# GpSimd's order between two blocks of a transformer layer, and scores for maxima one PSUM bank at a time

## The reference

```python
xn = _layernorm(x)
# attention over windows of 64 rows, 16 heads of 16 values, each window sees 3
scores = where(mask, einsum('bnqhd,bnkhd->bhnqk', q, kc) * scale, -1e9)
out = einsum('bhnqk,bnkhd->bnqhd', softmax(scores), vc) @ Wo + bo
h = layer_norm(out + xn, g1, b1)
f = gelu(h @ W1 + c1) @ W2 + c2
attn = layer_norm(f + h, g2, b2)
# routing: each row goes through the one expert with the largest score
chosen = argmax(xn @ gate_w.T)
moe = xn + xn @ expert_w[chosen].T
return x + attn + moe
```

## Time and profile before

| what | before |
|---|---|
| median of 3 runs (lowest to highest) | 1473.32 us (1461.51 to 1473.76) |
| the profiled execution | 1471.13 us, span 1469.3 us |
| PE busy | 1200.0 us, 82% |
| VectorE busy | 924.3 us, 63% |
| ScalarE busy | 726.5 us, 49% |
| GpSimd busy | 825.5 us, 56% |
| chain that ended last | PE 42%, GpSimd 26%, issue 12%, VectorE 7% |
| granted TensorE clock, mean | 0.928 |

### The profile page before, as it was taken

The page is one execution under the profiler, slowest core; times in us unless marked ns, Lnnn a source line. Parts: engine busy times, 40 slices in busy tenths (PEclk is TensorE's granted clock), DMA queues, the critical chain, the costliest instruction groups (busy, mean ns, idle before and its releaser), DMA issues.

```text
span 1469.3 us, 32444 instructions
## 1 busy us (share of the span) xinstructions
PE 1200.0 (82%) x11720; PEld 726.1 (49%) x11720; DVE 924.3 (63%) x2207; ACT 726.5 (49%) x1355; POOL 825.5 (56%) x1088
## 2 busy tenths in 40 slices
PE   0717898799879898898987898798986989878877
PEld 0414454554637445464545546374454645365445
DVE  8554657476656746776575766577474765656455
ACT  1304657146562574436572575526763365725661
POOL 6551568435781567625674457815676266834664
PEclk9958999899989899999998999898998999999989
DMA  8443081231723254230812327231532408122010
GB/s 250 120 130 116 31 199 50 80 127 44 163 76 104 73 132 99 72 125 31 199 51 80 126 59 156 69 109 67 147 85 72 124 32 202 54 85 87 3 29 29
DMA packets 93977, 142.89 MB, mean 97 GB/s; under 512 B 10592, under 2 KB 62688, under 8 KB 91744
## 3 DMA queue, kind: packets, MB, share of 16 engines
q1 hardware_dynamic: 87680, 124.04, 30.6%
q0 software_dynamic: 6144, 16.79, 3.6%
HBM read 74.47 MB, written 68.29 MB: 97 GB/s over the span
## 4 chain that ended last, share of the span: by engine, by line
PE 42%; POOL 26%; issue 12%; DVE 7%; ACT 3%; DMA 3%; another core or an unknown queue 0%; DVEq 0%; POOLq 0%; SPq 0%; ACTq 0%
PE bank L1180 6%; PE bank L1268 5%; PE bank L1078 5%; PE bank L1081 5%; PE bank L1079 5%; PE bank L1173 4%; POOL x_sb L521 4%; DVE m_sb L745 4%; POOL xs_dram L507 4%; POOL res_r L527 3%; POOL pool L496 3%; POOL pool L499 3%; POOL x_sb L483 3%; POOL x_sb L480 3%; PE bank L1148 2%
## 5 line engine op out<-in xcount | busy, mean ns | idle before, releaser
L981 ACT ACTIVATE pool<-bank 128x512 f32<-128x512 f32 x512 | 285.5, 596 | 150.9 <-PE bank L1180 147.5
L745 DVE TENSOR_REDUCE m_sb<-bank 128x2 f32<-128x384 f32 x512 | 261.5, 552 | 130.3 <-PE bank L1188 128.7
L468 POOL TENSOR_SCALAR_AFFINE_SELECT pool<-pool 128x512 f32<-128x512 f32 x256 | 183.6, 717 | 244.1 <-ACT pool L981 205.5
L1180 PE MATMUL bank<-q_s,k_s 128*128 128x256 f16 x1024 | 185.1, 289 | 15.7 <-ACT pool L981 8.8
L412 POOL TENSOR_TENSOR rs<-ve,neghalf 128x1 f32<-128x1 f32 x64 | 36.9, 577 | 251.7 <-DVE ve L806 251.7
L1268 PE MATMUL bank<-pool,v_a 128*32 128x256 f32 (+2 forms) x2560 | 166.7, 352 | 8.4 <-POOL pool L473 8.3
L970 ACT ACTIVATE xn<-bank 128x256 f32<-128x256 f32 x120 | 46.0, 384 | 224.4 <-PE bank L1081 218.6
L1173 PE MATMUL bank<-k_s,q_s 48*64 48x192 f16 x2048 | 99.1, 270 | 58.9 <-DVE m_sb L745 40.5
L1180 PEld LDWEIGHTS bank<-q_s,k_s 128*128 128x128 f16 x1024 | 82.5, 101 | 126.3 <-issue 97.4
L820 DVE TENSOR_TENSOR pool<-pool 128x512 f16<-128x512 f32 x128 | 105.5, 827 | 62.1 <-ACT pool L995 52.7
L473 POOL TENSOR_SCALAR_AFFINE_SELECT pool<-pool 128x512 f32<-128x512 f32 x208 | 133.4, 641 | 0.0
(11 more groups left out here) (154 smaller groups left out, 2644.6 us busy)
## 6 DMA issues: line engine op xcount, KB each, us to landing
pair_dram<-pool SPq DMA_DIRECT2D x96, 256.0 KB, 4.2
xn<-xs_dram SPq DMA_DIRECT2D x40, 384.0 KB, 3.6
ys_dram<-xn SPq DMA_DIRECT2D x120, 128.0 KB, 1.8
q_s<-pair_dram SPq DMA_DIRECT2D x32, 384.0 KB, 6.7
k_s<-pair_dram SPq DMA_DIRECT2D x32, 384.0 KB, 8.3
x_sb<-in_L_attn_x SPq DMA_DIRECT2D x8, 1024.0 KB, 5.8
res_dram<-x_sb SPq DMA_DIRECT2D x8, 1024.0 KB, 5.2
res_r<-res_dram SPq DMA_DIRECT2D x8, 1024.0 KB, 5.0
```

The source lines that it names most:

```text
L468: nc.gpsimd.affine_select(out=p, in_=p, compare_op=ALU.is_ge, fill=0.0, base=0, pattern=[[0, 4], [1, 2 * W]], channel_multiplier=-1).then_ ...
L745: nc.vector.tensor_reduce(m_sb[:, 4 * g + par:4 * g + 4:2, t], SB[par][:, 0:2 * WIN].rearrange("p (h c) -> p h c", h=2), AX.X, ALU.max).th ...
L981: nc.scalar.activation(prob[:, (k + 2) % 3, par::2, :], TB[par][:, :].rearrange("p (h q) -> p h q", h=2), ACT.Exp, scale=EXP_SCALE).then_i ...
L1180: return nc.tensor.matmul(out[:, i * QW:i * QW + QW], k_s[:, h, W + t * P:W + t * P + P], q_s[:, 2 * h + par, t * P:t * P + QW], start=Tru ...
```

## The change

It has four parts.

1. The two sums of x_sb (`residual`) move into the loop, one tile per step after the band of steps 14 to 29 (`residual_tile`). SyncE's `store_res` moves ahead of the last two stacked loads.
2. GpSimd's order after the loop becomes: the 8 gathers (`fetch`), `rstd`, `residual_attn`, the wait for the gathers and the 8 sums (`add_fetched`), `send`, `residual_mlp`.
3. In the loop, the scores for maxima are computed one bank at a time (`scores_half`): parity 1 after the first `scores_t`, parity 0 after the second. In the W1 and W2 stages `scores` stays as it was.
4. The transposed maxima of the four groups get banks MB[0], MB[1], MB[0] and SB[1], their wait is only for the maxima of their own group, and the scores no longer wait for them.

```diff
+    RES_AT = XN_AT + 4
-    MAX_STEPS = [LEAD - T + 3] + [T * g + MAX_AT - 1 + LEAD for g in range(G - 2)]
+        XB = [MB[0], MB[1], MB[0], SB[1]]
@@ SyncE, turn
                     for i in range(2, 4):
                         pair_stores(b + 1, i)
+                    store_res(b + 1)
                     for i in range(2, 4):
                         stack_loads(b + 1, i)
-                    store_res(b + 1)
@@ GpSimd
+            def residual_tile(b, i):
+                t = i % T
+                if i == 0:
+                    pool.wait_ge(xn_rdy.sem, xn_rdy.at(b, T))
+                    pool.sem_inc(passed, 1)
+                if i < T:
+                    nc.gpsimd.tensor_tensor(x_sb[:, t, :], x_sb[:, t, :], xn[:, t, :], ALU.add).then_inc(res_p.sem, 1)
+                else:
+                    pool.wait_ge(res_p.sem, res_p.at(b, t + 1))
+                    nc.gpsimd.tensor_tensor(x_sb[:, t, :], x_sb[:, t, :], bc[:, 3, :], ALU.add).then_inc(res_p.sem, 1)
@@ GpSimd, fetch cut in two before its wait
+            def add_fetched(b):
+
                 pool.wait_ge(res_in.sem, res_in.at(b, 16))
@@ GpSimd, turn
-                if not last:
-                    residual(b + 1)
+                    if RES_AT <= k < RES_AT + 2 * T and not last:
+                        residual_tile(b + 1, k - RES_AT)
+                fetch(b, last)
                 rstd(b, 1, ve1, rs1)
                 if not last:
                     residual_attn(b + 1)
-                fetch(b, last)
+                add_fetched(b)
@@ VectorE and PE, max_cols: SB[g % 2] becomes XB[g]
-                pe.wait_ge(mx.sem, mx.at(b, 2 * issued))
+                pe.wait_ge(mx.sem, mx.at(b, 2 * T * (g + 1)))
@@ PE, xn_transposes
+                if u == 0 and not first:
+                    pe.wait_ge(mT_ev.sem, mT_ev.at(b - 1, 3))
@@ PE, scores_wait
-                if j in MAX_STEPS and par == 1:
-                    pe.wait_ge(mT_ev.sem, mT_ev.at(b, MAX_STEPS.index(j) + 1))
-                    pe.sem_inc(passed, 1)
@@ PE
+            def scores_half(b, j, par):
+
+                scores_wait(b, j, par)
+                for i in range(2):
+                    for n in range(2):
+                        score_mm(SB[par], n, j, par, i)
+                for n in range(2):
+                    mm = mask_mm(SB[par], n, j % T, par)
+                mm.then_inc(S_ps.sem, 1)
@@ PE, turn
-                    if 1 <= k and k - 1 + LEAD < STEPS:
-                        scores(b, k - 1 + LEAD)
+                        if 1 <= k and k - 1 + LEAD < STEPS:
+                            scores_half(b, k - 1 + LEAD, 1 - par)
```

More of the change, by code:

```diff
@@ L474, in band @@
                                         pattern=[[0, 4], [-1, 2 * W]], channel_multiplier=1).then_inc(masked.sem, 1)
-            def residual(b):
[L478 to L483, removed]
+            def residual_tile(b, i):
[8 more added lines that the diff above has]
+                    nc.gpsimd.tensor_tensor(x_sb[:, t, :], x_sb[:, t, :], bc[:, 3, :], ALU.add).then_inc(res_p.sem, 1)
+            def residual(b):
+                for i in range(2 * T):
+                    residual_tile(b, i)
             def residual_attn(b, first=False):
@@ L749, in max_cols @@
                 dve.wait_ge(mT_ps.sem, mT_ps.at(b, g + 1))
-                nc.vector.tensor_scalar(mT[:, g, :], SB[g % 2][0:4 * T, 0:P], -1.0 / KONE, None,
+                nc.vector.tensor_scalar(mT[:, g, :], XB[g][0:4 * T, 0:P], -1.0 / KONE, None,
                                         ALU.mult).then_inc(mT_ev.sem, 1)
@@ L1221, in scores, with max_cols @@
                             mm.then_inc(S_ps.sem, 1)
-            def max_cols(b, g, issued):
-                pe.wait_ge(mx.sem, mx.at(b, 2 * issued))
-                nc.tensor.transpose(SB[g % 2][0:4 * T, 0:P], m_sb[:, 4 * g:4 * g + 4, :].rearrange("p h t -> p (h t)"),
+            def scores_half(b, j, par):
[6 more added lines that the diff above has]
+                mm.then_inc(S_ps.sem, 1)
+            def max_cols(b, g):
+                pe.wait_ge(mx.sem, mx.at(b, 2 * T * (g + 1)))
+                nc.tensor.transpose(XB[g][0:4 * T, 0:P], m_sb[:, 4 * g:4 * g + 4, :].rearrange("p h t -> p (h t)"),
                                     ident[:, :]).then_inc(mT_ps.sem, 1)
@@ L1359, in d_stage @@
                         if t == 3:
-                            max_cols(b + 1, 0, LEAD - T + t)
+                            max_cols(b + 1, 0)
                         scores(b + 1, LEAD - T + t)
@@ L1365, in turn @@
                     if k % T == MAX_AT and k < 3 * T:
-                        max_cols(b, k // T + 1, min(k - 1 + LEAD, STEPS))
+                        max_cols(b, k // T + 1)
                     for par in range(2):
@@ L1401, in _ @@
                 if t == 3:
-                    max_cols(0, 0, LEAD - T + t)
+                    max_cols(0, 0)
                 scores(0, LEAD - T + t, first=True)
```

## The result

| | before | changed |
|---|---|---|
| median of 4 runs each, on one chip | 1473.54 us | 1609.32 us (1600.41 to 1629.66) |
| ratio | | 1.091, interval 1.082 to 1.100 |
| profiled execution | 1471.13 us | 1629.66 us |
| granted TensorE clock, mean | 0.928 | 0.818 |

The changed kernel is 9% slower; the prediction said no change.

A forecast was written before the change was run, and what follows sets the result against it. Bounds: VectorE's W2 start waiting for GpSimd's last n1 sum (61.9 us over seven turns), and the loop. Sum: 24.5 - 3.5 - 1.4 (x_sb sums in the loop) - 18.1 + 4.3 = 5.8 us gained, median 1468 us, range 1440 to 1496.

The forecast's parts named there:

- Scores by bank: In the loop, halves cost 0.48 us more per step at full clock; 2.1 to 2.7 per turn, 18.1 us lost.
- Rival 4: In the loop, the halves' matmuls run one after another (0.96 us a step): about 1525 us; chance 0.08.
- GpSimd's order: Behind the loop, gathers ahead of the reciprocal root let W2 start earlier: at most 51.3 us, 24.5 gained after costs.
- (a): Gathers wait for the x_sb store, taken to land at 727, and delay root, n1 and W1 by 1.4 us a turn.
- (b): Sums into res_r beside VectorE's routing slow its two-input operations and hold back send: 1.9 us a turn (0.5 to 3).
- (c): Products and sums of n1 move beside W1's second half and stretch it by 1.1 us a turn (0 to 4).
- The floor behind it: Between VectorE's last low half of W1 and the first W2 sum, 2.8 us remain each turn.
- Own banks: In W2's tile 3, PE's 0.61 us wait for VectorE's copy of transposed maxima falls away: 4.3 us gained.
- The clock's 3.5 at the first tile: At W2's start, PE's remaining idleness may lower the clock for the first tile: 0.5 us a turn, 3.5 lost.
- 1: W1 isn't stretched: sums beside routing and n1 work beside W1 cost nothing, 22.8 us gained, 1450 us; chance 0.24.
- 2: In the loop, halves are cheap (0.2 us per step): 34 us better than forecast, 1434 us; chance 0.08.
- rival 3: The x_sb store lands late, at 731 behind the stacked loads, delaying the root: 29 us more, 1496 us; chance 0.13.

The follow-up runs named there:

- e7: Changed kernel with whole-block scores in steps 1 to 8 of each loop and halves in steps 9 to 18; ratio 0.982 against before.
- e1: Changed kernel with the loop's scores computed as whole blocks again, the other three parts kept; ratio 0.971 against before.
- e6: Changed kernel with scores split by pairs of heads, both blocks using all four array quarters, still five tile-form changes a step; ratio 1.008 against before.
- e8: Changed kernel with halves in steps 1 to 8 of each loop and whole-block scores in steps 9 to 18; ratio 1.024 against before.
- e5: Changed kernel with the two score halves one behind the other, both after the second transposed score; ratio 0.969 against before.
- e4: Kernel before with only the own banks for transposed maxima and the weaker waits; ratio 0.989 against before.
- e9: Changed kernel with each transposed score matmul (full array) issued twice in steps 1 to 5 of every loop; ratio 0.996 against before.
- e12: Changed kernel with the two score halves one behind the other, run again on another chip; ratio 0.967 against before.
- e10: Changed kernel with the first pair of score matmuls of each half (two quarters) issued three times more in steps 1 to 5; ratio 1.098 against before.

## Why the prediction was wrong

**The failed step is "Scores by bank"**, where it sums the turn. It took the low stretch at the loop's start as a given length ("Steps 1 to 4 lie in a stretch at half clock", +0.8) and had steps 5 to 10 at full clock behind it, at 2.0 us. The stretch became 51 to 68 us long, and these steps took 3.43. It took idleness as what brings the low level ("without the low clock if PE stays busy"), since the second low stretch lay behind a stop. Nothing in the rows of before showed what ends a low stretch. The loops were to become 19.5 us longer over the run, sums of x_sb included, and became 194.2 longer. Rival 4 had the right sign for another reason, and its mechanism (matmuls in sequence) did not occur: the four of a half take 0.35 us, as below.

The size per step at full clock, the term that I had worked out most closely, was right. Predicted were 2.0 for steps 5 to 10 and 2.58 for 15 to 17. e7 shows for halves 1.90 to 2.01 in steps 10 and 13, and 2.59 in 15 and 16. One step of e7 in turn 3:

```profile
667.76 0.39 PE L1193 MATMUL bank<-q_s,k_s 128*128 128x256 f16 x2
668.09 0.35 PE L1186 MATMUL bank<-k_s,q_s 48*64 48x192 f16 x4
668.27 0.28 PE L1201 MATMUL bank<-mask,ident 64*64 64x256 bf16 x2
668.48 0.39 PE L1193 MATMUL bank<-q_s,k_s 128*128 128x256 f16 x2
668.80 0.35 PE L1186 MATMUL bank<-k_s,q_s 48*64 48x192 f16 x4
668.99 0.27 PE L1201 MATMUL bank<-mask,ident 64*64 64x256 bf16 x2
669.20 0.64 PE L1288 MATMUL bank<-pool,v_a 128*32 128x256 f32 x8
```

Transposed scores and halves take 1.44 us (667.76 to 669.20), and with a whole block 0.95 (687.39 to 688.34): 0.49 more, where I took 0.48. With adjacent halves it is 1.06 (above), so 0.38 of the 0.49 is the price of standing apart.

**GpSimd's order** came out near the sum, though not term by term. From `b_stage`'s first matmul to the first W2 sum a full turn took 65.1 us on average before and takes 61.5 now, 25.3 less over seven turns; predicted were 24.5, less the 3.5 for the clock. Its steps, in turn 3 (GpSimd, then VectorE):

```profile
804.00 1.05 POOL L529 DMA_INDIRECT x_sb<-ys_dram,pos_y  x1 [7.38 <-DMA res_dram<-x_sb]
...
813.83 1.68 POOL L410 TENSOR_TENSOR rs<-ve,neghalf 128x8 f32<-128x8 f32 x1
815.51 5.50 POOL L497 TENSOR_TENSOR xnbo<-xn,bc 128x256 f32<-128x256 f32 x8
820.97 5.50 POOL L537 TENSOR_TENSOR res_r<-res_r,x_sb 128x256 f32<-128x256 f32 x8
831.53 1.05 POOL L515 DMA_INDIRECT xs_dram<-xn,pos  x1 [5.07 <-DVE pos L731]
...
841.82 5.49 POOL L504 TENSOR_TENSOR pool<-pool,bc 128x256 f32<-128x256 f32 x8
847.38 7.18 POOL L507 TENSOR_TENSOR pool<-pool,bc 128x256 f32<-128x256 f32 x8
```

```profile
842.78 6.21 DVE L831 TENSOR_TENSOR pool<-pool 128x512 f16<-128x512 f32 x2 [0.17 <-ACT pool L1006]
...
857.15 0.69 DVE L831 TENSOR_TENSOR pool<-pool 128x512 f16<-128x512 f32 x1 [1.55 <-ACT pool L1006]
...
859.61 0.42 DVE L809 SCALAR_TENSOR_TENSOR pool<-bank,pool 128x256 f32<-128x256 f32 x1 [0.50 <-PE bank L1092]
```

(a) The gathers waited for the store and pushed the root behind the variances, which were there at 812.24: 1.6 late, predicted 1.4. (b) Counted from the stage's start (720.9 before, 797.1 now), the positions came 2.9 us later, at 830.53; 1.6 of it is the root's, so (b) cost 1.3 instead of 1.9; of the two-input operations of one_hot only L691 paid (1.02 us, before 0.22 as L680). (c) The last low half ends 60.7 behind the start instead of 54.8, 5.9 later; less those 2.9, (c) cost 3.0 instead of 1.1, and one pair of L831, 6.21 us, shows where; one L831 of 5.1 us stands in five of the seven turns, none in e1. GpSimd ended at 854.56, 3.3 before the end of that low half, and the wait of 61.9 is gone from this turn; over the run 9.2 us of it are left, in two turns. The floor behind it is 1.8 us, predicted 2.8. Together 7.7 where I had 7.2: the misses nearly cancel, which was luck.

The new order has a price that I did not see, and that the changed kernel's profiled execution doesn't show. L804 (L793 before) takes two SBUF inputs and starts with the first of now 16 sums on GpSimd. In four turns (two of e6, one of e7, one of e8) it took 10.9 us, until the last of them was over. In e7, turn 0:

```profile
224.24 5.47 POOL L497 TENSOR_TENSOR xnbo<-xn,bc 128x256 f32<-128x256 f32 x8
229.68 5.47 POOL L537 TENSOR_TENSOR res_r<-res_r,x_sb 128x256 f32<-128x256 f32 x8
224.29 10.89 DVE L804 SCALAR_TENSOR_TENSOR nm<-mv,rs 128x8 f32<-128x8 f32 x1 [1.34 <-POOL rs L410]
```

Those turns need 71 to 73 us from the end of the loop's last exponential to the first W2 sum, the other full turns of these kernels 60 to 65. Over all kernels with this order the stretch gained between 2 (e1) and 30 us (e5), so the 25 is the figure of one execution.

**Own banks**: tiles 3 and 4 of W2 are 5.03 apart instead of 5.71, 0.68 times seven is 4.8, predicted 4.3. The clock's 3.5 at the first tile did not come: the first tile takes 4.27 us in five turns and 6.4 and 7.5 in two, before 4.6 to 4.7 in five and 6.1 and 6.4 in two, 0.8 less over the seven. The 6.4 and 7.5 lie in the two turns in which VectorE still waits for GpSimd's last sum. In e4 the loops are 15 us shorter than before, though part of that is given back behind them (5 and 6 us).

**Of the rivals**, 1 was not seen (W1 is stretched) and 2 is refuted by the 0.49. Counted from the stage's start, rival 3 has the store land 10.1 us behind it and my 727 is 6.1 behind it; it landed 6.9 behind.

## What to carry to other kernels

Before cutting a block of tiled matmuls into pieces, look at the granted clock of the stretch in which they run. A PE that is busy without a gap, but with part of its array, can stay at half clock for as long as that pattern lasts, and the same pattern started at full clock stays at full clock. So a low stretch at a stage's start is not a fixed cost: it can grow with the pattern behind it, and in this kernel tiled halves on different rows issued back to back, or even more full-array work, ended or avoided it.

## What the runs showed of the hardware that I had not expected

- **The clock has a memory.** The Trainium skill ("TensorE: Matmul & The Clock Gate", Part 1) says that sustained matmul activity releases the full clock. Here PE was busy 51 of 51 us and stayed at 0.50; if activity is read as the engine's busy time, the trace differs, and the measurement decides.
- **Doubling matmuls made a kernel faster**: the changed kernel takes 1.091 of before, and with 160 full-array matmuls more 0.996 (e9; each against before on its own chip).
- **Some executions have a stall that before has not.** In e1 PE stands still for 1.3 to 3.3 us, twelve times and 25 us in all, with "issue" as what ended it (it waited for nothing that the profile shows), mostly at the loop's end and in the stages behind it. Before and the changed kernel have one each of over 0.7 us, at the first step of the first loop. The timeline of PE in e1, turn 4, and its DMA queues at 860 to 872:

```profile
866.11 0.32 PE L1288 MATMUL bank<-pool,v_a 128*32 128x192 f32 x1 [3.31 <-issue]
```

```profile
q1 hardware_dynamic: 1537, 3.62, 104.4%
q8 instruction: 2, 0.03, 1.4%
```

In 864 to 866 PE, VectorE and ScalarE all do nothing, while the data queue fills the 16 DMA engines and two packets of instructions go over the same ones. 18.5 us of these stalls lie between a loop's end and the first W2 sum, where e1 lacks 27 of the 29 us gained. That instructions arrive late behind data would fit, but it was not tested. Nor do the stalls follow the kernel or its speed: e5 has 2 and e12, the same kernel, 12; e10, slower than before, has 8. e5 to e8, profiled on one chip, have 1 to 5; e9 to e12, on another, have 8 to 14.
